# RWKV chunk loop behind a cross-attention: the last sum of a chunk on VectorE with one store, instead of a stored residual and an accumulating store

## What is computed

```python
# cross-attention over 64 sequences of 64 channels x 256, batch norm over (batch, time), residual
x = gamma * (w_y - mean) * rsqrt(var + EPS) + beta + x_this
# RWKV block on x (64, 64, 256), heads H = 32 of S = 8
xn = ln(x); sx = token_shift(xn)
x5 = xn + sx * (maa_stack + lora(xn + sx * maa_x))       # five mixes: k, w, v, r, g
w, r, k, v, g = ...                                      # decay, receptance, key, value, gate
s_t = k_t v_t + w_t * s_{t-1};  out_t = r_t (u k_t v_t + s_{t-1})
x1 = x + (group_norm(out) * g) @ Wo.T                    # the residual "x1"
xn2 = ln(x1); sx2 = token_shift(xn2)
xk = xn2 + sx2 * ffn_maa_k;  xr = xn2 + sx2 * ffn_maa_r
rr = sigmoid(xr @ ffn_Wr.T); kk = square(relu(xk @ ffn_Wk.T))
out = x1 + rr * (kk @ ffn_Wv.T)                          # the last sum
```

## Time and profile before

| | |
|---|---|
| median of three runs | 703.38 us (702.08, 703.38, 706.02) |
| the profiled execution, its own time | 699.89 us |
| its span, first to last instruction | 698.0 us |
| mean granted TensorE clock | 0.971 of 2.4 GHz |
| second gating step ends, passes 1 to 7 | 316.79, 376.90, 436.33, 495.75, 555.40, 614.64, 668.71 us |
| residual stores on SyncE's queue (L606) | 7 of 512 KB, 7.5 us to landing |
| accumulating stores on GpSimd's queue (L669) | 7 of 512 KB, 9.3 us to landing |

### The profile page before, as it was taken

The page is one execution under the profiler, slowest core; times in us unless marked ns, Lnnn a source line. Parts: engine busy times, 40 slices in busy tenths (PEclk is TensorE's granted clock), DMA queues, the critical chain, the costliest instruction groups (busy, mean ns, idle before and its releaser), DMA issues.

```text
span 698.0 us, 9609 instructions
## 1 busy us (share of the span) xinstructions
PE 623.4 (89%) x2694; PEld 335.1 (48%) x2694; DVE 595.5 (85%) x902; ACT 390.9 (56%) x933; POOL 294.3 (42%) x210
## 2 busy tenths in 40 slices
PE   8999999979787859899899989989988998987887
PEld 5666666656332223354445435344543534444366
DVE  2999999974578998989997997999799799889853
ACT  3888888843443255476375555737546564353252
POOL 1111363001125283566629437564841945590020
PEclk9999999999999879999999999999999999998799
DMA  2433221202361542367266145616706540670020
GB/s 67 119 121 108 79 72 58 90 5 31 103 138 28 109 91 45 57 129 147 31 132 142 28 87 133 110 30 150 150 1 126 132 73 12 138 150 31 0 31 30
DMA packets 42445, 57.87 MB, mean 83 GB/s; under 512 B 4979, under 2 KB 25107, under 8 KB 42419
## 3 DMA queue, kind: packets, MB, share of 16 engines
q1 hardware_dynamic: 33008, 46.77, 29.3%
q0 software_dynamic: 9104, 10.77, 8.6%
q10 hardware_dynamic: 306, 0.02, 0.0%
HBM read 16.13 MB, written 7.86 MB: 34 GB/s over the span
## 4 chain that ended last, share of the span: by engine, by line
PE 26%; DVE 19%; issue 14%; POOL 7%; ACT 2%; DMA 1%; SPq 1%; DVEq 0%; POOLq 0%; ACTq 0%
DVE state L1455 9%; PE ps_c L874 7%; PE ps_a L789 6%; POOL state L656 3%; PE ps_c L789 3%; DVE vb L1460 2%; PE ps_att L854 2%; POOL x L680 2%; PE ps_a L812 2%; PE ps_a L817 2%; POOL xn L646 1%; DVE x L1415 1%; DVE sx L1533 1%; DVE bonus L1426 1%; DMA vb<-v 1%
## 5 line engine op out<-in xcount | busy, mean ns | idle before, releaser
L680 POOL TENSOR_TENSOR x<-x,xn 128x1024 f32<-128x1024 f32 x35 | 86.2, 2472 | 157.6 <-DVE x L1415 157.6
L1455 DVE TENSOR_TENSOR_SCAN state<-ps_w,state 128x512 f32<-128x512 f32 x128 | 145.8, 1199 | 0.2
L789 PE MATMUL ps_a<-x,wsq 128*128 128x512 f32 x256 | 122.1, 621 | 9.1 <-POOL x L680 6.5
L656 POOL TENSOR_TENSOR state<-vb,k 128x2016 f32<-128x2016 f32 x23 | 109.0, 4740 | 21.7 <-DMA vb<-v 10.6
L1460 DVE TENSOR_TENSOR vb<-state,r 128x2048 f32<-128x2048 f32 x32 | 104.9, 3278 | 1.7
L789 PEld LDWEIGHTS ps_a<-x,wsq 128*128 128x128 f32 x256 | 49.8, 200 | 69.9 <-issue 62.2
L1415 DVE SCALAR_TENSOR_TENSOR x<-ps_a,vec,sx 128x512 f32<-128x512 f32 x80 | 56.2, 745 | 26.3 <-PE ps_a L812 14.2
L310 ACT ACTIVATE probs<-ps_f,negmax 128x256 f32<-128x256 f32 x128 | 58.9, 472 | 1.6 <-DVE negmax L364 0.9
L812 PE MATMUL ps_a<-mix_t,w 64*128 64x512 f32 x128 | 49.6, 642 | 7.6 <-ACT mix_t L1157 5.2
L854 PE MATMUL ps_att<-vb,pick 128*32 128x512 f32 x256 | 36.5, 644 | 11.0 <-DVE vb L1460 11.0
L1113 ACT ACTIVATE zn<-wyz,rs 128x256 f32 (+1 forms) x60 | 31.1, 594 | 24.1 <-POOL rs L640 24.1
(11 more groups left out here) (213 smaller groups left out, 1271.1 us busy)
## 6 DMA issues: line engine op xcount, KB each, us to landing
vb<-v SPq DMA_DIRECT2D x120, 256.0 KB, 5.5
x<-in_x SPq DMA_DIRECT2D x32, 128.0 KB, 2.1
c<-in_ctx SPq DMA_DIRECT2D x32, 128.0 KB, 2.2
wyz<-in_x POOLq DMA_DIRECT2D x7, 512.0 KB, 5.8
out<-wyz SPq DMA_DIRECT2D x7, 512.0 KB, 7.5
out<-sx POOLq DMA_DIRECT2D x7, 512.0 KB, 9.3
vb<-v SPq DMA_DIRECT2D x16, 128.0 KB, 2.4
wsq<-in_wsq POOLq DMA_DIRECT2D x7, 256.0 KB, 3.4
```

Source lines behind the costliest of these rows:

```text
L656: nc.gpsimd.tensor_tensor(st[q][:, :, :, 1:L], src[:, :, :, 0:L - 1], wide(k[p][h][:, :])[:, :, :, 0:L - 1], ALU.mult).then_inc(kv_at(n, h ...
L680: nc.gpsimd.tensor_tensor(x5[j % 2][:, :, :], x5[j % 2][:, :, :], xn[:, :, 1:L1], ALU.add).then_inc(x5_ready, 1)
L789: mm = nc.tensor.matmul(bank[:, :], wsq[:, weight, c, P * o:P * o + P], src(c), start=(c == 0), stop=(c == EC - 1))
L1455: nc.vector.tensor_tensor_scan(row, w[h][:, :], row, 0.0, ALU.mult, ALU.add).then_inc(scanned, 1)
```

## The change

GpSimd's `add_out` and SyncE's `store_x1` go. VectorE gets two more steps behind the gating steps, `y = 0.5 * y + x1` in place (`c_final`), and SyncE's queue stores `y` at the place where it stored x1. The 0.5 moves out of the value weights into these steps (and into L1513 for the last chunk). `prev0` is loaded with the late weights; `stored` is set to 16 at the start by VectorE. The counts of `s_pick` go down by one.

```diff
-LATE = 37
+LATE = 38
@@ attention, GpSimd
-                             (t["prev1"], d["prev1"]))):
+                             (t["prev1"], d["prev1"]), (t["prev0"], d["prev0"]))):
...
-            nc.gpsimd.tensor_scalar(t["wsq"][:, FV, :, :], t["wsq"][:, FV, :, :], 0.5, 1.0, ALU.mult, ALU.mult).then_inc(s_pick, 1)
@@ rwkv, SyncE
-            def store_x1(n):
-                sp.wait_ge(x1_ready, n * 2 + 2)
-                sp.wait_ge(stored, n * 16 + 16)
-                sp.dma_start(out[bass.ds(n * TILES, TILES)].rearrange("a p f -> p a f"), wyz[:, bass.ds(n * TILES, TILES), :]).then_inc(x1_stored, 16)
+            def store(n):
+                sp.wait_ge(out_ready, n * 2 + 2)
+                sp.dma_start(out[bass.ds(n * TILES, TILES)].rearrange("a p f -> p a f"), y).then_inc(stored, 16)
@@ body of SyncE
                 if c:
-                    store_x1(n - 1)
+                    store(n - 1)
...
-            sp.wait_ge(x1_stored, 16 * CHUNKS - 16)
@@ rwkv, GpSimd
-            def add_out(n):
-
-                pool.wait_ge(y_mid, n * 2 + 4)
-                pool.wait_ge(x1_stored, n * 16 + 16)
-                pool.dma_start(out[bass.ds(n * TILES, TILES)].rearrange("a p f -> p a f"), y, accum_op=ALU.add).then_inc(stored, 16)
@@ body and last_pass of GpSimd
-                add_out(n - 1)
...
-            pool.dma_start(t["prev0"][:, :, :], d["prev0"]).then_inc(stored, 16)
...
-            pool.wait_ge(stored, 16)
@@ rwkv, VectorE
-                nc.vector.scalar_tensor_tensor(yi, yi, 1.0, wyz[:, END * TILES + 2 * i:END * TILES + 2 * i + 2, :], ALU.mult, ALU.add).then_inc(last_ready, 1)
+                nc.vector.scalar_tensor_tensor(yi, yi, 0.5, wyz[:, END * TILES + 2 * i:END * TILES + 2 * i + 2, :], ALU.mult, ALU.add).then_inc(last_ready, 1)
...
+            def c_final(n):
+                for i in range(2):
+                    dve.wait_ge(y_mid, n * 2 + i + 3)
+                    nc.vector.scalar_tensor_tensor(y[:, 2 * i:2 * i + 2, :], y[:, 2 * i:2 * i + 2, :], 0.5,
+                                                   wyz[:, bass.ds(n * TILES + 2 * i, 2), :], ALU.mult, ALU.add).then_inc(out_ready, 1)
@@ body and last_pass of VectorE
                 c_gate_value(n - 1)
+                c_final(n - 1)
@@ start of VectorE
             dve.sem_inc(y_mid, 2)
+            dve.sem_inc(stored, 16)
```

More of the change, by code:

```diff
@@ L188, in _ @@
             nc.gpsimd.tensor_copy(t["wsq"][:, WG, :, :].rearrange("p c o -> p (c o)"), wg_eh[:, :, :].rearrange("p a f -> p (a f)")).then_inc(s_pick, 1)
-            nc.gpsimd.tensor_scalar(t["wsq"][:, FV, :, :], t["wsq"][:, FV, :, :], 0.5, 1.0, ALU.mult, ALU.mult).then_inc(s_pick, 1)
-            for w_, at in ((2, 10), (1, 13)):
+            for w_, at in ((2, 9), (1, 12)):
                 nc.gpsimd.tensor_tensor(sum_v[:, :, 0:w_], sum_v[:, :, 0:w_], sum_v[:, :, w_:2 * w_], ALU.add).then_inc(s_pick, 1)
@@ L197, in _ @@
             nc.gpsimd.tensor_scalar(t["avg_eh"][:, :, :], sum_i[:, 0:1, :].broadcast_to([P, S, HH]), 1.0 / S, 1.0, ALU.mult, ALU.mult).then_inc(s_pick, 1)
-            pool.wait_ge(s_pick, 19)
+            pool.wait_ge(s_pick, 18)
             nc.gpsimd.tensor_tensor(wv, wv, sum_v[:, :, 0:1].broadcast_to([P, EC * H, S]), ALU.subtract).then_inc(s_pick, 1)
             nc.gpsimd.tensor_tensor(s0[:, :, :, :], s0[:, :, :, :], sum_s[:, :, 0:1, :].broadcast_to([P, 2, S, B]), ALU.subtract).then_inc(s_pick, 1)
-            pool.wait_ge(s_pick, 21)
+            pool.wait_ge(s_pick, 20)
         @block.tensor
@@ L459, in rwkv @@
     xn2_ready, xprev2, sx2_ready, xk_ready, xr_ready = sem("xn2_ready"), sem("xprev2_ready"), sem("sx2_ready"), sem("xk_ready"), sem("xr_ready")
-    relu_ready, kk_ready, rr_ready, y_mid, x1_stored, stored = sem("relu_ready"), sem("kk_ready"), sem("rr_ready"), sem("y_mid"), sem("x1_stored"), sem("prev0_in_and_out_stored")
+    relu_ready, kk_ready, rr_ready, y_mid, out_ready, stored = sem("relu_ready"), sem("kk_ready"), sem("rr_ready"), sem("y_mid"), sem("out_ready"), sem("out_stored")
     c_done = sem("c_matmuls_done")
```

## The result

| | before | changed |
|---|---|---|
| median of four runs each | 702.73 us (700.88 to 706.02) | 723.62 us (720.58 to 725.83) |
| ratio | | 1.0306, 95% interval 1.0267 to 1.0346 |
| profiled execution, span | 699.89, 698.0 us | 720.58, 718.9 us |
| mean granted TensorE clock, profiled | 0.971 | 0.964 |

What follows compares the result with a forecast made beforehand. VectorE was taken to set the pass. Terms 14.3 + 4.1 - 0.6 + 1.4 + 1.5 = 20.7 us, added to the 703.38 us median, gave 724 us (chance 0.79), range 712 to 734.

Steps and rivals of the forecast that it cites:

- VectorE sets the pass: Steady pass: VectorE busy 54.4 of 59 us; whatever is put behind its gating steps is added to the pass.
- the rival's sum: New steps get the port before GpSimd's multiplication: hand-over 8.2 us instead of 9.05, -6.5 in all, 697 us; chance 0.11.
- spared by accident: Hand-over of the old kernel: GpSimd waited for the gating steps, so its multiplication ran beside VectorE's scans.
- The hand-over: Second gating step to product: one new step waits out GpSimd's multiplication, +3.6 us at each of four, +4.1 at the fifth.
- The last pass: Sixth hand-over +3.7; late spread values keep GpSimd's second multiplication off the bonus steps, -4.3 (or 0); together -0.6 us.
- The tail: Last gating steps to L1467: the two new steps go in between, nothing big on GpSimd; +1.4 us.
- SyncE's queue: Second spread of v queued behind the new store lands later, but its reader is later too, 5.5 us of cover: cost 0.
- The clock: TensorE waits 3.0 us for the later bonus step and may drop to half clock: 0.3 in five passes, 1.5 us.

Runs made afterwards that it cites:

- waiting for the new steps: Changed kernel with GpSimd waiting for both new steps before it multiplies for the next pass; 702.76 us, 1.0035 of the kernel before.
- one SBUF input: Changed kernel with the gated value written back to its PSUM bank, so no gating or new step has two SBUF inputs; 702.35 us, ratio 1.0017.
- the early release: Kernel before without its accumulating store, no new steps on VectorE, gated value missing from chunks 0 to 6; 696.77 us, ratio 0.9937.
- the run with the other order: Changed kernel with the new store behind the eight transfers of the second spread in SyncE's queue, not in front; 726.37 us, ratio 1.038.

## Why the prediction was right

*What bounds.* "VectorE sets the pass" was right upward only. The kernel before stands at the knee of the table: longer hand-overs count fully, shorter ones don't. The forecast itself needed only the upward half. The step that failed is the rival's sum, in which each microsecond off VectorE was a microsecond off the pass (697 us for the case in which the new steps are not held up). The two kernels that make that case, waiting for the new steps and one SBUF input, ran 1.0035 and 1.0017 of the kernel before, which is no difference that these runs can tell.

*The old kernel was "spared by accident".* Right as to the new steps. But its product was held up by 2.26 to 1.47 us in each hand-over, and the early release shows that this cost at most 0.35 us of a steady pass.

*The hand-over.* Forecast 9.05 + 3.6; measured 12.14 to 12.22 in five of six, that is +3.1 or +3.2 in four and +3.6 in the fifth, +3.4 in the sixth, 19.5 in all where 22.1 was forecast. The term was sized 0.5 too large: the addition's end to the multiplication's end took 4.69 us instead of 4.9, and I had left out the overlap of neighbouring instructions, 0.08 us at each of several boundaries. Which of the two steps would be held up did not matter, as argued. (The prediction's 14.3 for 4 x 3.6 is a rounding of 0.1; nothing hangs on it.)

*The last pass.* -4.3 was forecast as its gain, about -1.7 came. The bonus step is free, as forecast. But GpSimd's second multiplication, which waits 13.65 us for the spread values, now holds the product of the second part. Timelines of GpSimd and VectorE of the changed kernel:

```profile
651.28 4.46 POOL L653 TENSOR_TENSOR state<-vb,k 128x2016 f32<-128x2016 f32 x1 [13.65 <-DMA vb<-v]
...
644.36 1.41 DVE L1413 SCALAR_TENSOR_TENSOR bonus<-r,vec,k 128x512 f32<-128x512 f32 x2
...
652.94 4.96 DVE L1447 TENSOR_TENSOR vb<-state,r 128x2048 f32<-128x2048 f32 x1
```

4.96 - 2.29 = 2.67 us are lost again. I had asked whether it would meet L1519 or nothing, and not what came behind the scans.

*The tail.* 1.4 forecast; 1.1 longer.

*SyncE's queue.* Cost 0, right for the steady passes: between 315 and 629 us GpSimd waits for no transfer, and the run with the other order gains nothing.

*The clock.* 1.5 us were taken, 0 to 8.5 named. In the steady passes TensorE now waits 2.5 us for the bonus step, where it did not wait before and 3.0 was forecast. In the fourth pass the granted clock then fell for 10 us. TensorE's timeline behind the first hand-over, and the table by stretch of the fourth pass (columns as in the earlier trace rows):

```profile
327.96 1.98 PE L833 MATMUL ps_a<-bonus,cst 128*128 128x512 f32 x4 [2.50 <-DVE bonus L1413]
...
503.00:517.50 14.50, 11.92 (x34) 5.49 (x33) 14.40 (x11) 11.42 (x16) 5.56 (x3) 1.00 0.56 131
517.60:527.70 10.10, 8.68 (x13) 2.84 (x12) 6.98 (x12) 1.72 (x2) 0.00 (x0) 0.50 0.38 70
527.80:569.00 41.20, 38.42 (x149) 19.51 (x148) 36.52 (x42) 20.60 (x50) 26.47 (x15) 1.00 0.34 64
```

That pass is 65.90 us. The one before it, at the full clock, is 62.57, and in the run with the other queue order the fourth pass, at the full clock and with the same hand-over, is 62.82: 3.1 to 3.3 us for one such fall to 1.2 GHz. The second and the fifth pass of the changed kernel, at a granted clock of 0.97 and 0.95, are longer too (0.5 and 1.1 us above 62.57); so is the first pass of the kernel before, at 0.97 (0.7 above 59.43). Over the five passes the growth of 19.9 us is more than the 16.2 by which their hand-overs grew; the difference of 3.7 is the term for which I took 1.5. This is part of what made up for the smaller hand-over term. In the four runs of the changed kernel the mean clock and the span go together: 0.964 and 718.9, 0.957 and 721.6, 0.952 and 722.3, 0.952 and 724.1. That the falls come from the longer wait is not shown. TensorE waits 2.50 to 2.58 us for the bonus step in each of the five passes, and the first and the third of them stayed at 1.00; the first pass of the kernel before fell to 0.97 without that wait. No run took the wait away and left the rest.

*The total.* 20.7 was forecast on the profile, 20.9 measured, with errors of -2.6 (hand-overs), +2.6 (last pass), +2.2 (clock), -0.3 (tail) and -1.8 (the first hand-over came earlier, where nothing was forecast). The last one looks like the scatter of one execution and not like the change: the second gating step there ends at 315.0 us here, and at 317.1, 320.3, 317.9 and 317.1 in the four variants with a wait, with one SBUF input and with the other queue order, which do the same work up to that point. That the errors cancel to within 0.2 us is luck; the mechanism and the 3% are not. No version that beats the kernel before came out of the runs: the two that cure the loss meet TensorE's chain.

## What to carry to other kernels

When a wait on one engine is removed, ask what that engine does next and beside which instructions of the other one it will now run; here a wait for bookkeeping, with the store's issue behind it, had put GpSimd's multiplication beside VectorE's scans and off the place where the new steps came. Where such a step is needed, let one operand stay in PSUM, or make GpSimd wait for all the steps of the group and not for the first ones. And before a microsecond on the busiest engine is counted, test on which side of the knee the kernel stands: lengthening and shortening the same stretch gave slopes of 1 and 0.

## What the runs showed of the hardware that was not expected

A waiting GpSimd did not have to wait for the end of a group of VectorE's steps, only for the end of one: with the first new step issued 0.16 us ahead of GpSimd's multiplication, the first took 0.69 and the second 4.97 us. A held-up instruction is shown as busy for all of its wait, so a busy share does not tell work from waiting: of the 33.3 us of the fourteen new steps only some 9.7 are work, by an estimate of fourteen times the 0.69 of an undisturbed one.

A plain store of 512 KB landed 3.4 us after its issue in the changed kernel (2.9 to 3.5, seven of them), where the same bytes took 7.5 (median) from the same queue, issued right behind the eight transfers of the first spread, and 9.3 as an accumulating store in the kernel before. No engine's wait list shows a steady pass waiting for any of the three.
